# Skipping the gather of unused rows by the bounds check in a graph convolution kernel

## What is computed

```python
def gcn_conv(x, W, b, src, dst, n_nodes):
    h = x @ W
    deg = segment_sum(ones_like(dst), dst, num_segments=n_nodes)
    dinv = where(deg > 0, rsqrt(deg), 0.0)
    norm = dinv[src] * dinv[dst]
    msgs = h[src] * norm[:, None]
    return segment_sum(msgs, dst, num_segments=n_nodes) + b

src, dst = add_self_loops(edge_index, n)
h = relu(gcn_conv(layernorm(x), W1, b1, src, dst, n))
x = x + gcn_conv(h, W2, b2, src, dst, n)
x = x + mixture_of_experts(layernorm(x))      # 32 experts, 32 slots each
```

## Time and profile before

| what | us |
|---|---|
| median of 3 runs | 3398.9 |
| lowest and highest of them | 3392.09, 3399.05 |
| span of the profiled execution | 3527.4 |
| `prepare`, first gather of the first layer | 0 to 219.2 |
| first layer, first to last gather issued | 219.2 to 1487.3 |
| second layer, first to last gather issued | 1542.8 to 2902.7 |

### The profile page before, as it was taken

The page is one execution under the profiler, slowest core; times in us unless marked ns, Lnnn a source line. Parts: engine busy times, 40 slices in busy tenths (PEclk is TensorE's granted clock), DMA queues, the critical chain, the costliest instruction groups (busy, mean ns, idle before and its releaser), DMA issues. The chain is left out here.

```text
span 3527.4 us, 56846 instructions
## 1 busy us (share of the span) xinstructions
PE 3143.9 (89%) x19474; PEld 2019.7 (57%) x19474; DVE 1942.6 (55%) x2983; ACT 1205.6 (34%) x1447; POOL 1842.0 (52%) x1754
## 2 busy tenths in 40 slices
PE   7237999999999999967999999999999998588998
PEld 7125666666666666634665656665656664244665
DVE  8773444444443444425777877777777775101332
ACT  6951222222222222213444444444444442011000
POOL 0146666666666666536676666776666661100000
PEclk9999999999999999979999999999999999799999
DMA  9488888888888888749998988988889987999996
GB/s 374 180 316 317 293 280 287 303 287 271 298 284 299 293 295 297 263 159 312 313 307 291 311 298 297 312 302 294 288 286 308 308 284 287 340 324 271 277 268 177
DMA packets 344441, 1018.61 MB, mean 289 GB/s; under 512 B 145314, under 2 KB 148668, under 8 KB 335984
## 3 DMA queue, kind: packets, MB, share of 16 engines
q0 software_dynamic: 135776, 660.85, 56.5%
q1 hardware_dynamic: 196916, 322.85, 27.3%
q10 hardware_dynamic: 11484, 31.39, 2.8%
HBM read 854.14 MB, written 135.08 MB: 280 GB/s over the span
## 5 line engine op out<-in xcount | busy, mean ns | idle before, releaser
L1299 POOL DMA_INDIRECT xs<-table,idx x833 | 914.2, 1097 | 501.3 <-PE m_part L1476 214.0
L821 POOL DMA_INDIRECT xs<-table,idx x833 | 878.8, 1055 | 442.9 <-issue 202.9
L1073 PE MATMUL a_part<-xs 128*128 128x512 f16 (+1 forms) x3332 | 592.1, 332 | 76.1 <-DMA xs<-table,idx 52.5
L1476 PE MATMUL m_part<-xs 128*128 128x512 f16 (+1 forms) x3332 | 591.9, 332 | 55.7 <-DMA xs<-table,idx 19.2
L1053 PE MATMUL a_ps_o<-Ws,xs 128*128 128x512 f16 x3528 | 593.1, 326 | 8.9 <-issue 5.5
L1073 PEld LDWEIGHTS a_part<-xs 128*128 128x128 f16 x3332 | 416.3, 142 | 213.2 <-issue 96.9
L1476 PEld LDWEIGHTS m_part<-xs 128*128 128x128 f16 x3332 | 419.3, 142 | 198.4 <-issue 77.3
L1053 PEld LDWEIGHTS a_ps_o<-Ws,xs 128*128 128x128 f16 x3528 | 344.9, 98 | 236.8 <-issue 12.6
L1505 PE MATMUL m_ps_l<-xs,m_xT 128*128 128x512 f16 x1764 | 391.6, 380 | 8.0 <-issue 7.9
L1492 PE MATMUL m_ps_s<-dw_mem,xn_mem 128*128 128x512 f16 x1296 | 312.2, 380 | 3.5 <-DVE xs L1365 3.0
L1505 PEld LDWEIGHTS m_ps_l<-xs,m_xT 128*128 128x128 f16 x1764 | 172.2, 98 | 219.2 <-issue 16.8
(11 more groups left out here) (377 smaller groups left out, 3770.9 us busy)
## 6 DMA issues: line engine op xcount, KB each, us to landing
xs<-in_L_ffn_w_dram SPq DMA_DIRECT2D x64, 1152.0 KB, 11.3
xs<-table SPq DMA_DIRECT2D x98, 384.0 KB
xs<-table,idx POOLq DMA_INDIRECT x1666
cw_dram<-xs SPq DMA_DIRECT2D x49, 512.0 KB
x_pad<-xs SPq DMA_DIRECT2D x7, 2688.0 KB, 23.9
table<-arena SPq DMA_DIRECT2D x49, 384.0 KB, 4.5
table<-xs SPq DMA_DIRECT2D x49, 384.0 KB
xs<-x_pad SPq DMA_DIRECT2D x49, 384.0 KB
```

Of the source, the lines that this page charges most:

```text
L821: pool.indirect_dma_start(out=ring[:, t, :], out_offset=None, in_=table, in_offset=bass.IndirectOffsetOnAxis(ap=idx[:, k:k + 1], axis=0)). ...
L1073: mm = nc.tensor.matmul(part[:, bass.ds(to + a, z - a)], pick[:, i % 2, :, t], ring[:, n % RING, half * D + a:half * D + z], start=False, ...
L1299: pool.indirect_dma_start(out=ring[:, t, :], out_offset=None, in_=table, in_offset=bass.IndirectOffsetOnAxis(ap=idx[:, n:n + 1], axis=0)). ...
L1476: mm = nc.tensor.matmul(part[:, bass.ds(off + at, e - f)], pick[:, i % 2, :, t], ring[:, n % RING, half * D + f:half * D + e], start=False ...
```

## The change

All places without an edge of their block get a row number beyond the table, and the gathers of both layers are given a bounds check: a row number above 6271 (`NBR * P - 1`) is skipped, nothing is copied for it and the place of the ring keeps what it held.

In `prepare`, `far` is computed from `work2`: (w + 1 - 128) * w is above zero exactly where w is below 0 or above 127, and there `far` becomes 2 to the power 20. It is added to the source numbers in `work` before they are transposed. Two things are exempt: the places 0 of all tiles (the sum runs over 1 to 127), and the first 32 tiles (`FULL`), in which `far` is set to zero; these fill the rings of both layers with rows once. `far` shares its memory with `lo16` and `hi16`, which have been used by then.

```diff
--- before.py
+++ after.py
@@ -28,6 +28,8 @@
 ZERO_ACC = 2
 SPARE_ACC = 3
 NOWHERE = 200
+BEYOND = 2 ** 20
+FULL = 32
 FAR = 4096.0
 HT = 16
 NX = 32
@@ -195,14 +197,16 @@
         total = sb("total", [P, NBR], F32)
         nmean = sb("nmean", [P, NBR], F32)
         squares = sb("squares", [P, NBR], F32)
-        lo16 = sb("lo16", [P, QC * P], F16)
-        hi16 = sb("hi16", [P, QC * P], F16)
+        codes16 = sb("codes16", [P, 2 * QC * P], F16)
+        lo16 = codes16[:, 0:QC * P]
+        hi16 = codes16[:, QC * P:2 * QC * P]
         iota_j = sb("iota_j", [P, P], F16)
         arena = sb("arena", [P, TR * 2 * D], F16)
         oh_lo = arena[:, 0:2 * P * HT].rearrange("p (s n t) -> p s n t", s=2, t=HT)
         oh_hi = arena[:, 2 * P * HT:2 * (P + NBR) * HT].rearrange("p (s n t) -> p s n t", s=2, t=HT)
         unused = arena[:, 2 * (P + NBR) * HT:2 * (P + NBR) * HT + 2 * D].rearrange("p (s d) -> p s d", s=2)
         stage = arena[:, :].rearrange("p (s d) -> p s d", s=TR)
+        far = codes16[:, :].bitcast(F32).rearrange("p (q e) -> p q e", q=QC)
         ones16 = sb("ones16", [P, P], F16)
         zeros16 = sb("zeros16", [P, P], F16)
         diff = sb("diff", [P, P], F32)
@@ -657,7 +661,12 @@
                 for q in range(QC):
                     last = v.tensor_scalar(work2[:, q, :], raw_dst[:, q, :], bk128[:, q:q + 1], None, ALU.subtract)
                 last.then_inc(tiles_f, 1)
-                v.tensor_copy(work[:, :, :], raw_src[:, :, :]).then_inc(tiles_f, 1)
+                v.wait_ge(tiles_f, 1)
+                link(v.scalar_tensor_tensor(far[:, :, :], work2[:, :, :], 1.0 - P, work2[:, :, :], ALU.add, ALU.mult))
+                link(v.tensor_scalar(far[:, :, :], far[:, :, :], 0.0, float(BEYOND), ALU.is_gt, ALU.mult))
+                link(v.tensor_copy(work[:, :, :], raw_src[:, :, :]))
+                link(v.memset(far[0:FULL, 0, :], 0.0))
+                v.tensor_tensor(work[:, :, 1:P], work[:, :, 1:P], far[:, :, 1:P], ALU.add).then_inc(tiles_f, 1)
                 low_halves(24, 28)
                 normalise(41)
                 v.wait_ge(tiles_t, 1)
@@ -819,7 +828,8 @@
                     t = k % RING
                     wait(pool, consumed, k - RING + 1)
                     pool.indirect_dma_start(out=ring[:, t, :], out_offset=None, in_=table,
-                                            in_offset=bass.IndirectOffsetOnAxis(ap=idx[:, k:k + 1], axis=0)).then_inc(gathered[t], 16)
+                                            in_offset=bass.IndirectOffsetOnAxis(ap=idx[:, k:k + 1], axis=0),
+                                            bounds_check=NBR * P - 1, oob_is_err=False).then_inc(gathered[t], 16)
 
             @block.scalar
             def _(act):
@@ -1297,7 +1307,8 @@
                     t = n % RING
                     wait(pool, consumed, n - RING + 1)
                     pool.indirect_dma_start(out=ring[:, t, :], out_offset=None, in_=table,
-                                            in_offset=bass.IndirectOffsetOnAxis(ap=idx[:, n:n + 1], axis=0)).then_inc(gathered[t], 16)
+                                            in_offset=bass.IndirectOffsetOnAxis(ap=idx[:, n:n + 1], axis=0),
+                                            bounds_check=NBR * P - 1, oob_is_err=False).then_inc(gathered[t], 16)
 
             @block.scalar
             def _(act):
```

## The result

The changed kernel takes 3410.5 us (median of 5 runs, 3406.22 to 3412.3), the kernel before 3396.1 us in the same session (5 runs, 3392.09 to 3399.05). The ratio is 1.0038, with an interval of 1.0026 to 1.0049: the change makes the kernel **slower by 0.38%**, some 14 us. That is more than the 0.2% that can be told. The forecast was 3402.9 us and "no difference" (3392 to 3406, with 68%); what came is the sign of the rival "small costs add up" (3409 us). The time lies within the range, 3389 to 3428.

What follows compares the result with a forecast made beforehand. The prediction took PE to bound both layers. From 3398.9 us it added 2 us for `prepare` and 2 us for the layers' starts, less 0 for transfers: 3402.9 us, no difference (3392 to 3406, 68%); range 3389 to 3428.

Steps and rivals of the forecast that it cites:

- small costs add up: Rival, 7%: DVE detour lost in full (3.4 us), both layers' starts suffer at +0.15 us; slower by 7 to 15 us, 3409 us.
- PE bounds both layers, the transfers don't: Both layers: PE never waits for a gather in steady state, so moving fewer bytes gains nothing there.
- The change's 39 MB: Gathers of both layers: skipped rows remove 39 MB, 6% of the queue's 660.85 MB; worth taken as 0, ends 0 and 15 us.
- POOL's reserve of 0.19 us per gather in the first layer: First layer, steady state: 1.53 - 1.04 - 0.305 us; added POOL time below this falls into POOL's waits for PE.
- The check's price of +0.07 us (ends -0.06 and +0.4): POOL, each gather of both layers: one register move and the check add 0.07 us, below both layers' reserves.
- The starts, 2 us: Starts of both layers: the 0.07 us per gather costs 2 us together, ends 0 and 14 us.
- Its steady part: Second layer, steady state: POOL's reserve of 0.24 us a gather takes in the check, so the pace stays as it is.
- `prepare`, 2 us (0 to 3.4): `prepare`: four added DVE instructions make a detour of up to 3.4 us, partly hidden; 2 us taken as lost.
- POOL becomes the bound: Rival, 16%: in both layers the check exceeds POOL's reserve, from +0.19 us on; 3545 us at +0.3, 3710 us at +0.4.
- the range's upper end: Whole kernel: 3428 us, taking in small costs and a check of +0.2, up to +0.22 us, where POOL begins to bound.
- the -0.06 us for 6% fewer descriptors: POOL's gathers, lower end of the check's price: the check costs nothing and 6% fewer descriptors are written.

## Why the prediction was right or wrong

*PE bounds both layers, the transfers don't: right.* Halving the gathers' bytes gained nothing, by skipping (3410.5 us, as the changed kernel) or by asking for half (3399.7 against 3396.5). The change's 39 MB were forecast and seen, and their worth was 0, as taken. From 400 to 900 us the kernel before moved 312 GB/s with 3395 matmuls of PE, the two others 162 GB/s with 3363 and 172 GB/s with 3386. How many GB/s this core can move at most no run shows. PE is busy for all of those 500.00 us in the kernel before, with 24.1 us of matmuls in a bin of 24.15, and for 1000.00 of 1000 us in the second layer.

*POOL's reserve of 0.19 us per gather in the first layer: wrong, and this is the step that failed.* It was the difference of a period of 1.53 us and 1.04 + 0.305 us of work, both read from an execution 131 us longer than the medians. In that one PE's transposes waited 38.7 us for DVE, 2.0 us in the same stretch of the kernel profiled again, and POOL looked idle beside a slower PE. At the pace of the medians PE takes a gather every 1.421 us, and gather and issue are 1.413. All that was left is what the long gathers give back, 0.052 - 0.020 = 0.032 us (below), and the check goes over that: in 400 to 900 us the gathers come 500 / 349 = 1.433 us apart. The prediction named the longer span and used it only for scaling "a term of a few us by a tenth of one". But the extra time wasn't spread evenly: from first to last gather the first layer took 1268.1 us and not 1188.6, 6.7% more, which is 0.11 us of the period. The mean gather, 1.04 us where it is 1.108, made up the rest. What slowed that execution no run shows.

Why doesn't +0.052 us on a full POOL cost 0.052 x 833 = 43 us? The long gathers give most of it back. In 400 to 900 us the mean gather went from 1.108 to 393.63 / 349 = 1.128 us, +0.020 only, though each common gather is 0.052 longer. For the 391 gathers of bins 7 to 29 that makes 8 us, some of it bridged by the ring. From bin 30 on POOL's mean did not grow at all (243.39 us for 219 gathers from 1090 to 1400 us in both kernels). The stand beside DVE fits this: it ended with the DVE instruction, so a gather that began later stood for less. The gathers over 0.04 us above the median are 239 in the kernel before and 182 in the changed one, and the excess over the median falls from 148 us to 116, 32 of the 43 us.

Why then do the bins up to about 30 pay at all? There DVE has one instruction more in most bins, for `phi`, which the second layer reads (lines 957 to 973; the last begins at 976.6 us). In the kernel before (profiled again) 17 gathers begin beside lines 957, 968 and 973, all with at most 0.12 us of them left, and none is long. The changed kernel:

```profile
887.07 1.22 DVE L983 SCALAR_TENSOR_TENSOR xs<-xs 128x1024 f16<-128x1024 f32 x1
887.15 2.00 POOL L830 DMA_INDIRECT xs<-table,idx  x1 [0.31 <-issue]
...
911.12 1.00 POOL L830 DMA_INDIRECT xs<-table,idx  x1 [0.30 <-issue]
911.17 1.22 DVE L983 SCALAR_TENSOR_TENSOR xs<-xs 128x1024 f16<-128x1024 f32 x1
```

The first gather begins 0.08 us after the instruction and stands for a whole microsecond; a bin later it begins 0.05 us before, and doesn't. In the six profiles with a check in the early bins 9 to 12 gathers stand so, 7.8 to 10.1 us together over the 0.946; in the six without it none or one does, but for the 64 row numbers, where nine take 1.02 to 1.04 us, 0.8 us together over the 0.946 and at most 1.0 us in any of the six. That is about what the check costs in the first layer, and it fits that the same check costs nothing from bin 30 on. By this the price hangs on which DVE instruction the gathers happen to begin beside, which other delays change as well: in the long execution of the kernel before, without any check, 14 gathers stand so. No run moved the `phi` work away to test this by itself.

*The check's price of +0.07 us (ends -0.06 and +0.4): right in size, wrong in kind.* It is 0.052 us, in the gather itself. I had put it on the register move, which costs nothing (0.998 us and 3410.2 us without it in the loop). That a comparison is small beside the writing of descriptors was my estimate; no run shows the time of either.

*The starts, 2 us: too low.* From the first gather to the last tile's matmul the first layer takes 1200.5 to 1203.6 us in the six profiles without a check in its early bins (the one with the one-hot built twice left aside) and 1208.2 to 1211.0 in the six with it; the means are 1201.8 and 1209.7, **+7.9 us**. Some 2 us of it are in its beginning: between 200 and 300 us the three profiles with an early check and nothing new on DVE have 231 to 234 matmuls, the six with neither 236 to 264. On average that is 16 fewer, at 0.147 us each. The spread is wide: PE still waits for single gathers there, and its granted clock over these 100 us is 0.85 to 0.93 in ten of the thirteen profiles and 0.70 to 0.73 in three. The rest comes in lumps when the ring's lead is used up. After the first bins PE takes 24.1 us for a bin in all twelve, but for bin 12, and in those with the check single bins take up to 2.4 us more: at the end of bin 5 they are 1.7 us behind the others on average, at bin 18 2.1, at bin 29 5.8, at bin 32 7.7, and hardly more after it.

For the second layer the same distance is 1324.8 to 1326.8 us in the five profiles with a check, 1326.0 on average. Of the eight without one six have 1321.8 to 1323.4, but two have 1325.7 and 1326.1 (the check in the first layer only, and the 64 row numbers); the mean is 1323.2. So **+2.8 us**, and less firmly than in the first layer. Its steady part was forecast right: PE's pace is unchanged, and the 0.052 us fall into POOL's idle time.

*`prepare`, 2 us (0 to 3.4): right.* The first gather starts at 221.0 to 222.0 us in the four profiles with the DVE instructions and at 219.0 to 219.9 in the nine others, +2.2 us between their means. The durations forecast, 1.1, 0.6, 0.1 and 1.1 us, were 1.09, 0.63, 0.17 and 1.08.

The new sum is 7.9 + 2.8 + 2.2 = 12.9 us; measured are 14.3. The forecast's own sum was 4. The single runs don't add up as well as the profiles: 7.8 and 3.1 us for the layers one by one, but 8.0 us for the check in both, and with DVE's -0.8 us some 5 to 7 us are missing from the 12.4 to 14.3 us of the three kernels that have everything. Each interval is some 3 us to either side, so what stays open is how these few us are shared out, not that the check makes most of them. The rival that had this sign told of the starts at +0.15 us and the detour in full; the true mechanism, a reserve that isn't there in the middle of the first layer, is the rival "POOL becomes the bound", at a far smaller price than the 0.19 us from which I let it decide. That the time lies in the range all the same is partly luck: the range's upper end was made from a check of 0.2 us on a reserve of 0.19, and what came was one of 0.052 on 0.032.

A gather's time hardly went by the number of its rows: with 64 row numbers in place of 128 it goes from 0.946 to 0.904 us, 4% for half, and with half of the rows skipped it stays at 0.998. So nothing is seen of the -0.06 us for 6% fewer descriptors. The starts were not costless: the check alone left the queue's packets at 135,776, as before, and made the median gather 0.052 us longer.

No experiment gave a version faster than the kernel before. All of the change's gain is in a resource that nobody waits for.

## What to carry to other kernels

Before a reserve is read as a difference (period less work), compare the span of the profiled execution with the unprofiled medians, and where it is longer, ask whose waits make it so: here a queue's waits of 1.18 us for another engine shrank to 0.30 us of issue time at the true pace. Two engines can be full at once, and 5% more per instruction on the one that isn't the bound was paid in part here: 7.9 us of the first layer's 43. Where an instruction's mean is well above its median, ask what ran on the other engines when the long ones began: here one view of POOL and DVE side by side tells it. In this kernel skipping rows by a bounds check saved bytes (39.45 MB) and nothing else, and every gather paid 0.052 us for it. What it is worth where transfers are waited for no run shows.

## What the runs showed of the hardware

All of it is from this kernel's two layers; "before" is the kernel before, profiled again, and medians are of 833 gathers of a layer.

- With the bounds check the median gather of 128 row numbers took 0.998 us, without it 0.946 (before), +0.052: with nothing skipped (the check alone), with 6% of the rows skipped (the changed kernel), with half of them skipped, and with the bound put into a register once.
- With 64 row numbers the median gather took 0.904 us, with 128 it took 0.946 (before). With 0.305 us of issue that is a period 0.04 us shorter than 1.25.
- In the first layer before, 238 gathers that began beside a DVE instruction ended 0.812 to 0.824 us after it (median 0.819), 233 of them beside the five instructions of the table above. In the changed kernel 181 such gathers ended 0.866 to 0.889 us after it (median 0.872), and with 64 row numbers the median is 0.774. In the changed kernel one gather began 0.08 us into an instruction and took 2.00 us; another began 0.05 us before the same instruction of the next bin and took 1.00. In the first layer before, 145 of the 148 us by which gathers exceed their median lie in those 238.
- Beside a reduction and a reciprocal no gather was long. In the second layer before, 45 gathers began beside line 1438 (a sum over 1024 elements, 1.22 us) with 1.09 us of it left or more, and 44 beside line 1439 (a reciprocal, 0.35 us) with 0.24 us left or more.
- The skipped rows left packets. With half of the rows skipped the queue moved 334 MB less (660.85 to 326.87), that is 108,700 rows, and its packets were 135,776 as before; 54,364 more of all packets were under 512 bytes (145,314 to 199,678), one for two skipped rows. With 64 row numbers, where the rows weren't asked for, the queue had 84,512 packets.
- Between two gathers POOL had 0.305 us (161.2 / 529 before). A register move of 0.029 us in it (the changed kernel, 175.9 / 577) left it at 0.305, and with a memset of 0.09 us in it a gather still began 1.25 us after the one before, and the kernel took 3396.3 against 3396.4 us.
- The page's line of bytes read from HBM has 854.14 MB before, in the changed kernel and with half of all rows skipped, but 539.18 MB with 64 row numbers. Whether skipped rows are read and dropped or the line counts what was asked for stays open.
